# Causal attention: in every third step off the diagonal, the last head's zero mask moves from VectorE to ScalarE and GpSimd

## The reference, cut to what matters

```python
scores = jnp.einsum('bhsd,bhtd->bhst', q, k) / math.sqrt(float(DH))
mask = jnp.tril(jnp.ones((S, S), dtype=scores.dtype))
scores = scores * mask
scores = jnp.where(scores == 0.0, -jnp.inf, scores)
attn = jax.nn.softmax(scores, axis=-1)
out = jnp.einsum('bhst,bhtd->bhsd', attn, v)
```

## Time and profile before

| | |
|---|---|
| median of 3 runs | 2426.57 us (2424.32 to 2427.54) |
| the profiled execution | 2427.19 us, of which 2425.5 us is the span of the trace |
| VectorE busy over the span | 1835.7 us (76%) |
| ScalarE busy | 1275.1 us (53%) |
| TensorE busy | 2071.2 us (85%) |
| GpSimd busy | 686.9 us (28%) |

### The profile page before, as it was taken

The page is one execution under the profiler, slowest core; times in us unless marked ns, Lnnn a source line. Parts: engine busy times, 40 slices in busy tenths (PEclk is TensorE's granted clock), DMA queues, the critical chain, the costliest instruction groups (busy, mean ns, idle before and its releaser), DMA issues. The chain is left out here.

```text
span 2425.5 us, 39929 instructions
## 1 busy us (share of the span) xinstructions
PE 2071.2 (85%) x10413; PEld 879.4 (36%) x10413; DVE 1835.7 (76%) x2435; ACT 1275.1 (53%) x1553; POOL 686.9 (28%) x1065
## 2 busy tenths in 40 slices
PE   5886888888888988888888899568799599999997
PEld 4441222212221222222222221356455355677775
DVE  2876999989999989999899999458679663333332
ACT  0555888877888878888788888222212111111110
POOL 0563111112111121111111111127536647233333
PEclk8897999999999999999999999789899799999999
DMA  3353221203121222212030000332000023453442
GB/s 119 130 170 103 40 37 20 29 12 51 20 29 20 29 43 35 33 20 29 13 93 12 13 9 3 110 124 87 0 0 0 6 97 110 115 115 93 103 99 34
DMA packets 124638, 133.70 MB, mean 55 GB/s; under 512 B 35257, under 2 KB 118930, under 8 KB 123792
## 3 DMA queue, kind: packets, MB, share of 16 engines
q1 hardware_dynamic: 109904, 117.96, 19.5%
q0 software_dynamic: 14592, 14.08, 3.3%
HBM read 96.95 MB, written 50.63 MB: 61 GB/s over the span
## 5 line engine op out<-in xcount | busy, mean ns | idle before, releaser
L914 DVE SCALAR_TENSOR_TENSOR arena<-ps_s,arena 128x1024 f32<-128x1024 f32 (+3 forms) x1152 | 1229.1, 1129 | 84.1 <-ACT arena L886 65.4
L886 ACT ACTIVATE arena<-ps_s 128x1024 f32<-128x1024 f32 (+3 forms) x1152 | 1043.7, 951 | 280.4 <-PE ps_s L792 266.4
L792 PE MATMUL ps_s<-arena 128*128 128x512 bf16 (+3 forms) x2304 | 645.8, 369 | 150.4 <-DVE arena L914 98.7
L817 PE MATMUL ps_o<-arena 128*32 128x512 f32 (+3 forms) x4608 | 578.9, 575 | 16.5 <-POOL arena L950 16.0
L792 PEld LDWEIGHTS ps_s<-arena 128*128 (+1 forms) x2304 | 174.3, 97 | 839.2 <-issue 708.5
L945 POOL COPY arena<-values 128x64 f32 x576 | 134.9, 237 | 877.0 <-PE ps_o L817 865.3
L1932 ACT ACTIVATE arena<-g_ps_g 128x320 f32<-128x320 f32 (+1 forms) x96 | 42.0, 437 | 308.9 <-PE g_ps_u L1866 308.9
L2117 POOL DMA_INDIRECT out<-values,slot_ids x80 | 123.4, 1542 | 238.9 <-DVE values L2081 210.6
L2054 DVE TENSOR_TENSOR arena<-g_ps_u,arena 128x320 f32<-128x320 f32 (+1 forms) x96 | 47.1, 491 | 166.7 <-ACT arena L1932 166.7
L817 PEld LDWEIGHTS ps_o<-arena 128*32 128x32 f32 x4608 | 91.2, 108 | 197.2 <-issue 145.0
L950 POOL TENSOR_SCALAR_AFFINE_SELECT arena<-arena 128x512 f32<-128x512 f32 x128 | 81.4, 636 | 242.8 <-DVE arena L914 242.8
(11 more groups left out here) (208 smaller groups left out, 1930.7 us busy)
## 6 DMA issues: line engine op xcount, KB each, us to landing
arena<-parts_dram SPq DMA_DIRECT2D x320, 64.0 KB, 3.0
parts_dram<-arena SPq DMA_DIRECT2D x32, 384.0 KB, 3.3
arena<-parts_dram SPq DMA_DIRECT2D x24, 512.0 KB, 7.1
slots_in_dram<-in_empty_slots SPq DMA_DIRECT2D x10, 1040.0 KB, 19.7
arena<-slots_in_dram SPq DMA_DIRECT2D x16, 650.0 KB, 4.4
arena<-in_L_ffn_w_gate SPq DMA_DIRECT2D x16, 352.0 KB, 3.1
arena<-in_L_ffn_w_up SPq DMA_DIRECT2D x16, 352.0 KB, 3.6
arena<-in_L_attn_x SPq DMA_DIRECT2D x8, 512.0 KB, 3.8
```

The costliest lines, as they stand in the source:

```text
L792: last = pe.matmul(ps_s[:, (2 * step.slot + pair) % 3, h, step.w0:], m.k_stack[:, bass.ds(head, 1), bass.ds(step.kt * P, P)].rearrange("p ...
L817: last = pe.matmul(ps_o[32 * h:32 * h + 32, step.j % 2, step.w0:], v_pad[:, step.slot, h], probs[:, step.slot, h, step.w0:], start=step.fi ...
L886: act.activation(probs[:, step.slot, 2 * pair:2 * pair + 2, step.w0:], ps_s[:, (2 * step.slot + pair) % 3, :, step.w0:], ACT.Exp, scale=1. ...
L914: dve.scalar_tensor_tensor(p, ps_s[:, (2 * step.slot + pair) % 3, :, step.w0:], 0.0, p, ALU.not_equal, ALU.mult).then_inc(bank, 1)
```

## The change

In a step off the diagonal whose slot is 0 (here called a shared step), VectorE masks only three heads. The fourth head's scores are copied by ScalarE to `o_raw` in SBUF, GpSimd turns them there into ones and zeros, and then multiplies the head's exponentials by them. The shared steps of block j are those with (2j(j+1) + k) % 3 == 0 and k < 4j: 0, 1, 3, 4, 5, 7, 8 and 9 in the blocks 0 to 7, 37 in a group and 148 in all.

```diff
+SHARED = 0
+def shares_in(j, kt):
+    return sum((2 * j * (j + 1) + k) % 3 == SHARED for k in range(min(kt, TT * j)))
...
 # TensorE
 def score(step, pair):
                 pe.wait_ge(bank, u + 1)
+                if pair == 0 and step.slot == (SHARED + 2) % 3:
+                    pe.wait_ge(scores_out, step.shares + 1)
...
 def weigh(step):
                     pe.wait_ge(bank, 2 * n + 5)
+                    if step.shared:
+                        pe.wait_ge(last_masked, step.shares + 2)
...
 # ScalarE, in emit, behind the two exponentials of the step
+                if step.shared:
+                    act.wait_ge(last_masked, step.shares + 1)
+                    act.wait_ge(o_turned, step.g * NB + step.j)
+                    act.activation(o_raw, ps_s[:, (2 * step.slot + 1) % 3, 1], ACT.Copy).then_inc(scores_out, 1)
...
-            def copy_out(j, weighed):
+            def copy_out(j, weighed, shares):
                 act.wait_ge(probs_free, weighed)
+                act.wait_ge(last_masked, shares + 1)
...
 # VectorE
-                    p = probs[:, step.slot, 2 * pair:2 * pair + 2, step.w0:]
-                    dve.scalar_tensor_tensor(p, ps_s[:, (2 * step.slot + pair) % 3, :, step.w0:], 0.0, p,
+                    heads = 1 if step.shared and pair == 1 else 2
+                    p = probs[:, step.slot, 2 * pair:2 * pair + heads, step.w0:]
+                    dve.scalar_tensor_tensor(p, ps_s[:, (2 * step.slot + pair) % 3, 0:heads, step.w0:], 0.0, p,
                                              ALU.not_equal, ALU.mult).then_inc(bank, 1)
...
-                dve.wait_ge(o_turned, unit)
+                dve.wait_ge(o_turned, unit + 1)
...
 # GpSimd, behind the copy of the values
+                if step.shared:
+                    hold(m, pool, scores_out, step.shares + 2)
+                    p = probs[:, step.slot, HG - 1]
+                    pool.tensor_scalar(o_raw, o_raw, 0.0, 0.0, ALU.is_equal, ALU.is_equal).then_inc(kept, 1)
+                    hold(m, pool, kept, step.shares + 1)
+                    pool.tensor_tensor(p, p, o_raw, ALU.mult).then_inc(last_masked, 1)
```

More of the change, by code:

```diff
@@ L96, in __init__, with shared, shares_until @@
         self.count = g * STEPS + self.n0 + kt
+        self.shares = g * SHARES + shares_until(j - 1) + shares_in(j, static_kt) + (0 if loop_kt is None else loop_kt)
+    @property
+    def shared(self):
+        return self.diag is None and self.slot == SHARED
 STEPS = sum(TT * (j + 1) for j in range(NB))
+SHARED = 0
+def shares_in(j, kt):
+    return sum((2 * j * (j + 1) + k) % 3 == SHARED for k in range(min(kt, TT * j)))
+def shares_until(j):
+    return sum(shares_in(i, TT * i) for i in range(j + 1))
+SHARES = shares_until(NB - 1)
 def walk(eng, emit):
@@ L701, in phase_attend @@
         recip_done = sem("recip_done")
+        scores_out, kept, last_masked = sem("scores_out"), sem("kept"), sem("last_masked")
         q_in = [sem("q_in0"), sem("q_in1")]
@@ L777, in _ @@
             pe.sem_inc(scored, 1)
+            pe.sem_inc(o_turned, 1)
             pe.wait_ge(consts, 1)
@@ L836, in following @@
                     nxt.count = step.count + 1
+                    nxt.shares = step.shares + step.shared
                     return nxt
@@ L870, in preceding @@
                 p.count = step.count - 1
+                p.shares = step.shares - p.shared
                 return p
@@ L880, in _ @@
         def _(act):
+            act.sem_inc(scores_out, 1)
             def emit(step):
@@ L888, in emit @@
                                    scale=1.0 / DH ** 0.5).then_inc(exped, 1)
+                if step.shared:
+                    act.wait_ge(last_masked, step.shares + 1)
+                    act.wait_ge(o_turned, step.g * NB + step.j)
+                    act.activation(o_raw, ps_s[:, (2 * step.slot + 1) % 3, 1], ACT.Copy).then_inc(scores_out, 1)
                 if step.diag == 1 and step.j > 0:
-                    copy_out(step.j - 1, step.g * STEPS + steps_until(step.j - 1) + 3)
+                    copy_out(step.j - 1, step.g * STEPS + steps_until(step.j - 1) + 3, step.shares)
                 if step.diag == 1 and step.j == 0:
                     with act.If(step.g > 0):
-                        copy_out(NB - 1, step.g * STEPS + 3)
-            def copy_out(j, weighed):
+                        copy_out(NB - 1, step.g * STEPS + 3, step.shares)
+            def copy_out(j, weighed, shares):
                 act.wait_ge(probs_free, weighed)
+                act.wait_ge(last_masked, shares + 1)
                 act.activation(o_raw, ps_o[:, j % 2], ACT.Copy).then_inc(o_copied, 1)
@@ L900, in _ @@
                 walk(act, emit)
-                copy_out(NB - 1, NG * STEPS + 3)
+                copy_out(NB - 1, NG * STEPS + 3, NG * SHARES)
         @block.vector
@@ L938, in _ @@
         def _(pool):
+            pool.sem_inc(last_masked, 1)
             pool.memset(v_pad[:, :, :, DH + 1:], 0.0)
```

## The result

| | before | after |
|---|---|---|
| median | 2426.2 us | 2904.3 us (2901.9 to 2911.3, 4 runs) |
| ratio | | 1.198, 95% interval 1.195 to 1.200 |
| span of the profiled execution | 2425.5 us | 2902.4 us |
| TensorE busy | 2071.2 us | 2208.5 us |
| VectorE busy | 1835.7 us | 1776.5 us |

The change costs 478 us, 3.23 us for each of the 148 shared steps. The forecast was 63 us more, 2490, in a range of 2455 to 2550: right in the sign and in the place, far off in the size.

The account below looks back on a forecast made before the run. A loop of mask, scores, weighing and exponential was taken as the bound, VectorE close behind. Later weighings cost 0.40 us per three steps, 59 us over 148, plus 4 behind blocks: 63 more, 2490 us, range 2455 to 2550.

Parts of the forecast that it names:

- The ring and its path: Loop of mask, scores, weighing, scores, exponential: 4.67 us per two steps; with the change three steps take 7.42 against 7.02.
- Removed, VectorE's 0.53: VectorE's last mask in a shared step shrinks from 1.22 to 0.69 us, 148 times, 78 us of its time.
- ScalarE's copy, 0.59, ending at 0.49: ScalarE's added 128x512 copy from PSUM takes 0.59 us and ends 0.49 behind the end of pair 1's exponential.
- The second chain of 7.23: Copy, two exponentials and masks to the next scores: three steps take 7.23 us without GpSimd time, 31 us more overall.
- GpSimd's tensor_scalar at 0.64: GpSimd's added compare, without a row, priced like the affine_select of 128x512: 0.64 us, between 0.24 and 1.16.
- The rival with a dearer GpSimd: GpSimd's compare costs 1.16 like a two-input instruction: three steps take 7.94 us, kernel 2567 us; chance 0.15.
- The product at 1.16: GpSimd's added 128x512 tensor_tensor on the last head's exponentials takes 1.16 us, 1.60 in its worst case.
- the handovers at 0.17, 0.18, 0.05: Waits on the way to the weighing: 0.17 us to GpSimd, 0.18 between its two instructions, 0.05 to TensorE.
- the blocking by VectorE: VectorE excluding GpSimd on a shared SBUF port pair; VectorE's masks read one operand from PSUM, so none priced.
- Removing 78 us by the highest occupancy: Rival: VectorE, busy 96.5%, was the bound, so 78 us come off and the kernel takes 2349; faster: chance 0.04.
- the signs listed to look for: Expected in the profile: busy sums of VectorE down 78 us, ScalarE up 88, GpSimd up 266; three steps in 7.4.

Follow-up runs that it names:

- five kernels: Changed kernel with arithmetic for compares, 2526 us; one compare, scores fourfold, 2650.9; scores sixfold, 2727.6; GpSimd's instructions out, 2454.5; that with VectorE masking both heads, 2455.3.
- The sixth: The changed kernel with one compare instead of two and the scores before a shared step's weighing made six times over; 2705 us.
- the 12 needless repeats: Changed kernel with scores before a shared step's weighing made six times, also in 12 places without a shared step (160 repeats instead of 148); 2727.6 us.
- the arithmetic run: The changed kernel with x * 1 + 0 instead of the two compares in GpSimd's tensor_scalar; 2526 us, ratio 1.041.

## Why the prediction was right in the sign and wrong in the size

- *The ring and its path*: right. With the measured durations and handovers and a full clock it gave 2520, 2647, 2713, 2458 and 2454 for five kernels that took 2526, 2651, 2728, 2454.5 and 2455.3. The sixth, 2647 against 2705, had work added that stood in the path itself.
- *Removed, VectorE's 0.53*: the duration was right (0.69 for the short form). It is worth 14 us by itself and nothing beside the copy.
- *ScalarE's copy, 0.59, ending at 0.49*: right (592 ns, 0.48). The second chain of 7.23 was 7.21.
- *GpSimd's tensor_scalar at 0.64, "at most the 1.16 of a two-input instruction of its own size"*: **the step that failed.** It measured 1.94. I took the price from instructions of the same shape, and the upper end from shape too; the price follows the operation. 1.30 x 148 = 192 us. The rival with a dearer GpSimd had the right place with a price that was too small (1.16, 2567 us).
- *The product at 1.16, the handovers at 0.17, 0.18, 0.05*: they measured 1.27, 0.20, 0.18, 0.14: 0.23 x 148 = 34 us. The product kept within 1262 to 1275 ns over its 148 times, so the blocking by VectorE for which the prediction priced nothing does not show in it.
- *The clock*: **the step that was missing.** All of TensorE's durations were taken from stretches at a granted clock of 1.00, while the forecast itself put a growing idle gap ahead of each weighing. With the scores repeated 177 us came off, and some 190 by the estimate that the 12 needless repeats cost 13.
- The sum: 63 forecast + 192 + 34 + 190 = 479, against 478 us measured. That it closes to 1 us is luck; the 63 and the 190 are good to a few us only.
- *"Removing 78 us by the highest occupancy"*: the Trainium skill's "Perfetto Trace Analysis", section Identifying the Most-Contended Engine, ranks engines by busy share. VectorE did have the highest, but 78 us less of it brought 14. Here the measurement decides.
- Of the signs listed to look for, the busy sums came out as -59 us for VectorE (forecast -78: the lengths of its masks do add up to 77 less, but the busy sum counts overlapping ends once, and in the full masks these overlaps fell from 60 to 38 us when it idled between them), +61 for ScalarE (+88; line 922 alone is 87.6) and +456 for GpSimd (+266, the compare).

## What to carry to other kernels

When work moves to an engine whose result another engine waits for, write down the path from the last common event to the consumer, in us, before and after; the busy shares of the engines don't show it. Take a duration from a row only if operation and shape agree, and leave the upper end open where the operation has no row. And where a change puts an idle gap ahead of TensorE's work, look at what the granted clock did behind gaps of such a length: the matmuls behind it may take longer too.

## What was not expected of the hardware

- On GpSimd a 128x512 tensor_scalar in place took 0.62 us with two arithmetic operations, 1.48 with one `min`, 1.50 with one `is_equal`, 1.94 with two. The Trainium skill, "GPSIMD Engine Reference", section Engine selection, calls one-input work on GpSimd roughly line-rate. That fits the arithmetic run (0.62 us, beside 0.69 for VectorE's mask of the same shape) and not the others, and the measurement decides.
- Idle gaps of TensorE ahead of a shared step's weighing, 2.6 us in the median, brought the lower clock in 104 of 120 stretches of the changed kernel. With gaps of 1.8 us in the median (one compare) it came in 35 of 120, and with 0.8 (two arithmetic operations) in 6 of 120.
- 2.2 us of useless matmuls in each shared step made the changed kernel 177 us faster.
